# Shared products, shared additions and the first expert units in one fixed order; in the first layer half of the expert weights are loaded behind the base stores

## What is computed

```python
x = x + 0.5 * ffn(layernorm(x))
x = x + attention(layernorm(x))
x = x + 0.5 * ffn(layernorm(x))

def moe(x, router_w, w_gate, w_up, w_down, ws_gate_up, ws_down):   # E = 64 experts, K = 8, F = 96, C = 64
    probs = softmax(x @ router_w.T)
    topk_w, topk_ids = top_k(probs, K);  topk_w /= sum(topk_w)
    # each expert takes its first C tokens in token order, the others are dropped
    g = einsum('ecd,edf->ecf', xb, w_gate);  u = einsum('ecd,edf->ecf', xb, w_up)
    y = einsum('ecf,efd->ecd', silu(g) * u, w_down)
    routed = segment_sum(y[slot of (token, expert)] * topk_w, token)
    gu = x @ ws_gate_up;  shared = silu(gu[:, :SF]) * gu[:, SF:] @ ws_down   # SF = 96
    return routed + shared
```

## Time and profile before

| | us |
|---|---|
| median of 3 runs | 890.02 |
| lowest and highest of them | 889.1, 890.67 |
| the profiled execution, its whole time | 890.89 |
| the span of its trace | 889.1 |
| first layer: start of the first and of the last unit's scatters | 87.67, 187.08 |
| second layer: the same | 774.02, 874.78 |

### The profile page before, as it was taken

One profiled execution on the slowest core, in us unless ns is written; L12 is line 12 of the kernel. 1 busy time (PEld: TensorE's weight loads), 2 busy tenths in 40 slices (PEclk: granted clock), 3 DMA queues, 4 the chain that ended last, 5 costly groups with the idle time before them and its releaser, 6 DMA issues.

```text
span 889.1 us, 17025 instructions
## 1 busy us (share of the span) xinstructions
PE 675.8 (76%) x5060; PEld 310.2 (35%) x5121; DVE 606.8 (68%) x1572; ACT 461.0 (52%) x1060; POOL 389.1 (44%) x509
## 2 busy tenths in 40 slices
PE   4886567503799999999999999999970388577650
PEld 3644444402133333333333333332220264354430
DVE  4877644344978888888888888888813569754430
ACT  5742222201177777777777777777773675222310
POOL 5546787676431331331331331330004655677762
PEclk9996778655599999999999999999995559657865
DMA  6996443243424444444444444434110131544324
GB/s 185 254 232 188 78 72 62 37 103 63 89 56 99 91 84 100 86 82 100 84 83 100 85 82 101 85 81 102 26 36 18 37 89 52 146 79 66 62 33 107
DMA packets 233724, 80.26 MB, mean 90 GB/s; under 512 B 166888, under 2 KB 226440, under 8 KB 233608
## 3 DMA queue, kind: packets, MB, share of 16 engines
q1 hardware_dynamic: 212936, 64.94, 33.0%
q0 software_dynamic: 12288, 10.49, 8.1%
q10 hardware_dynamic: 8448, 4.20, 1.6%
HBM read 49.94 MB, written 31.49 MB: 92 GB/s over the span
## 4 chain that ended last, share of the span: by engine, by line
PE 49%; issue 11%; DVE 9%; POOL 8%; DMA 7%; ACT 7%; another core or an unknown queue 1%; POOLq 0%; ACTq 0%; SPq 0%; DVEq 0%
PE psum L1453 14%; PE psum L1444 12%; PE psum L1431 10%; DMA sums<-sums_sb,sidx 6%; ACT arena L1203 5%; POOL sums L623 4%; PE psum L1263 1%; PE psum L1407 1%; PE psum L1265 1%; POOL arena L600 1%; PE psum L1272 1%; PE psum L1393 1%; PE psum L1249 1%; PE psum L1421 1%
## 5 line engine op out<-in xcount | busy, mean ns | idle before, releaser
L984 DVE TENSOR_REDUCE arena<-psum 128x2 f32<-128x1024 f32 x256 | 308.8, 1220 | 53.1 <-PE psum L1431 50.2
L1203 ACT ACTIVATE arena<-psum 128x512 f32<-128x512 f32 x512 | 282.1, 600 | 116.1 <-PE psum L1444 105.7
L1431 PE MATMUL psum<-arena 126*128 126x512 bf16 x512 | 198.8, 395 | 8.9 <-DVE arena L984 4.5
L1444 PE MATMUL psum<-arena 128*128 128x512 bf16 x451 | 173.2, 387 | 7.1 <-ACT arena L1203 3.4
L1453 PE MATMUL psum<-arena 128*32 128x512 f32 x1024 | 136.2, 604 | 1.3 <-ACT arena L1194 1.3
L679 POOL CAST arena<-arena 128x256 bf16<-128x256 f32 x32 | 12.7, 396 | 264.9 <-issue 260.9
L623 POOL DMA_INDIRECT sums<-sums_sb,sidx x64 | 102.9, 1607 | 58.5 <-DVE sums_sb L919 33.1
L1444 PEld LDWEIGHTS psum<-arena 128*128 128x128 bf16 x512 | 50.7, 100 | 150.1 <-ACT arena L1203 122.3
L919 DVE COPY sums_sb<-psum 128x256 f32<-128x256 f32 x32 | 13.6, 425 | 95.5 <-DMA sums<-sums_sb,sidx 55.7
L600 POOL DMA_INDIRECT arena<-dispatch_rows,arena x64 | 64.8, 1013 | 20.7 <-issue 18.3
L1431 PEld LDWEIGHTS psum<-arena 126*128 126x128 bf16 x512 | 49.6, 99 | 37.8 <-DVE arena L984 15.0
(11 more groups left out here) (138 smaller groups left out, 1095.8 us busy)
## 6 DMA issues: line engine op xcount, KB each, us to landing
arena<-qk_parts SPq DMA_DIRECT2D x128, 96.0 KB
ctx<-arena SPq DMA_DIRECT2D x32, 256.0 KB, 2.0
qk_parts<-arena SPq DMA_DIRECT2D x32, 192.0 KB, 3.8
dispatch_rows<-xn_sb ACTq DMA_DIRECT2D x16, 256.0 KB, 2.3
arena<-lists SPq DMA_DIRECT2D x16, 256.0 KB
sums<-x_sb SPq DMA_DIRECT2D x16, 256.0 KB
arena<-qk_parts SPq DMA_DIRECT2D x64, 64.0 KB
arena<-ctx SPq DMA_DIRECT2D x64, 64.0 KB, 2.4
```

What stands on the lines that cost most here:

```text
L984: dve.tensor_reduce(mx_r[r % 2][:, 2 * p:2 * p + 2], src, X, ALU.max).then_inc(a_mx, 1)
L1203: act.activation(p_r[tau % NPB], bank[4 + tau % 2][:, :], ACT.Exp, scale=SCALE).then_inc(a_P, 1)
L1431: ins = pe.matmul(bank[tau % 4][:, :], heads(q_st[r], rows, g)[:, qt * P:(qt + 1) * P], heads(k_st[r], rows, g), start=True, stop=True)
L1444: pe.matmul(bank[4 + tau % 2][:, :], keys, heads(q_st[r], rows, g), start=True, stop=True)\
```

## The change

It does five things, in both layers unless said otherwise.

1. POOL takes `shared_add(0)` to `shared_add(4)` from DVE. They stand between the products: `shared_mul(g)`, then `shared_add(g - 2)`. DVE keeps groups 5, 6 and 7, with a semaphore of their own. `shared_mul(0)` moves ahead of the last group's `weights`.
2. POOL's gathers all stand behind the products and additions. Six are issued, then POOL waits until PE has finished `gate_up(1)`, then two more; `ahead(q)` is 8 + 2q, so twelve units have gathers behind their scatters.
3. PE's `places(0)` moves behind `up(7)`, and `places(1)` one unit earlier.
4. DVE's order in the unit stage: `match` ahead of `hidden` and of `sum_copy`, `merge_blocks(1)` ahead of the loop, the other list steps a unit earlier and behind `pick`. `match` gets a third buffer `same`.
5. First layer only: the expert weights are loaded in slices of eight experts (gate, up, down). The first twelve transfers (experts 0 to 31) go between the stores of routing; the other twelve are issued by SP behind the base stores and `load_rows(1)`. PE waits for the first twelve before the units and for the others before `gate_up(4)`. The loads of the attention weights move from ahead of `load_rows(2)` to behind it.

The diff, cut to its core:

```diff
-        same = [carve(3 * P) for _ in range(2)]
+        same = [carve(3 * P) for _ in range(3)]
...
-                w, t = ((w_gate, wgu_sb[:, :, 0:F]), (w_up, wgu_sb[:, :, F:2 * F]), (w_down, wd_sb))[c // 8]
-                part = slice(c % 8 * E // 8, (c % 8 + 1) * E // 8)
+                w, t = ((w_gate, wgu_sb[:, :, 0:F]), (w_up, wgu_sb[:, :, F:2 * F]), (w_down, wd_sb))[c % 3]
+                part = slice(c // 3 * E // 8, (c // 3 + 1) * E // 8)
...
-                        expert_weights(2 * g)
-                        expert_weights(2 * g + 1)
+                        for c in range(12 * g // NG, 12 * (g + 1) // NG):
+                            expert_weights(c)
                     store_w(NG - 1, 1)
-                    for c in range(2 * NG, 24):
-                        expert_weights(c)
...
                 for c in range(1, 4):
-                    if c == 2 and f.p == 0:
+                    if c == 3 and f.p == 0:
                         attention_weights()
                     wait(sp, f.gtp, 2 * c - 1)
                     load_rows(c)
+                    if c == 1 and f.p == 0:
+                        for w in range(12, 24):
+                            expert_weights(w)
...
+                def shared_add(g):
+                    wait(pool, f.shy, g + 1)
+                    xs = x_sb[:, g * GT:(g + 1) * GT, :]
+                    pool.tensor_tensor(xs, xs, z_sb[:, g * GT * P:(g + 1) * GT * P].rearrange("p (i d) -> p i d", i=GT),
+                                       ALU.add).then_inc(f.shx.sem, 1)
...
+                    if g == NG - 1:
+                        shared_mul(0, 0)
                     weights(g, g % 2)
...
-                gather(0)
-                shared_mul(NG - 2, 0)
-                gather(1)
-                shared_mul(NG - 1, 1)
-                ahead = lambda q: min(NP2, 10 + 2 * q)
-                for k in range(2, ahead(0)):
+                ahead = lambda q: min(NP2, 8 + 2 * q)
+                for k in range(6):
+                    gather(k)
+                wait(pool, f.gu, 2)
+                for k in range(6, ahead(0)):
                     gather(k)
...
-                    wait(dve, f.sm, q - 1)
+                    wait(dve, f.sm, q - 2)
...
-                places(0)
                 up(NG - 2, 0)
                 down(NG - 3, 1)
                 up(NG - 1, 1)
+                places(0)
...
+                    if q == 4:
+                        pe.wait_ge(s_wexp[1], 16 * 12)
```

71 lines of the change are left out of this document (37 added, 34 removed).

## The result

| | kernel before | changed kernel |
|---|---|---|
| median, first comparison (20 runs each) | 890.94 us (886.71 to 894.07) | 893.15 us (890.47 to 898.3) |
| ratio, 95% interval | | 1.0032 (1.0017 to 1.0047) |
| second comparison (run 5 below): ratio | | 1.0050 (1.0033 to 1.0067) |
| spans of two traces each | 889.1, 888.4 us | 889.4, 891.9 us |

The changed kernel is slower, by 0.3 to 0.5%. The forecast was 884.4 us, with a range from 880.0 to 892.5. The changed kernel's first profiled execution took 891.11 us and lies on its quick side; the second, at 893.64, is close to its medians (893.15 and 893.03). Those of before took 890.89 and 890.13, the first at its median of the first comparison (890.94), both above its medians in the later ones (886 to 888 us).

What follows compares the result with a forecast made beforehand. POOL's scatters and gathers were taken to pace the two expert layers' units (6.42 us a period); first scatters, gathers, stalls and collision sum to -5.6 us, from the median of 890.0 to 884.4 us, range 880.0 to 892.5.

Steps and rivals of the forecast that it cites:

- The late weights: First layer: last twelve transfers, 4.7 MB, take 16 to 19 us, end at about 93, covered before `match(4)` and `gate_up(4)`.
- The collision: First layer: scatters of units 0 and 1 run beside full DMA engines, +1.5 us.
- rival 2: First layer: weights under 220 GB/s make list rows late for `match(4)`; at 150 GB/s unit 2 waits about 10 us, 894; chance 0.10.
- ACT's wait for `silu(1)`: Before the first scatters, both layers: ACT's idle 5.00 and 4.03 us ahead of `silu(1)` was taken as gone.
- the sum: Both layers: first scatters -3.3 and +0.8, gathers +0.6 twice, stalls -3.0 and -2.8, collision +1.5: -5.6 us.
- My path of 18.8 us: Both layers: from indices ready to the first scatters, 18.8 us, so scatters start at 84.4 and 774.8.
- Rival 1: Both layers: ACT's wait before `silu(1)` stays, first scatters 2.2 and 2 to 6.4 us later; 888.6 to 893; chance 0.22.
- Contention of list steps: List stage: DVE's short steps wait for POOL, 3 to 4.5 us per list; indices 4.2 us later in second layer.
- The merge ahead of the first `sum_copy`: Before the first scatters, both layers: the merge comes into the path, 2.85 us.
- Stalls of units 1 and 3: Unit stage: their waits for `sum_copy` beyond the 0.3 us gap go, -3.0 us first layer, -2.8 second.
- Eight gathers ahead: Unit stage: one more period has gathers, +0.6 us per layer; about 1 us of slack before the scatters.
- rival 3: Unit stage: eight gathers ahead are too few, 0.4 us more in each of 24 periods; 894; chance 0.05.

Runs made afterwards that it cites:

- run 5: The changed kernel again, unaltered, timed against the kernel before: ratio 1.0050 (1.0033 to 1.0067).
- runs 10: Changed kernel with POOL's five additions back on DVE: 1.0078 of before; the same with all weights ahead and the merge behind the first `sum_copy`: 0.9971.
- run 11: The kernel before with only the five additions moved to POOL, between its products: ratio to before 1.0085 (1.0057 to 1.0112).
- Run 9: Changed kernel with all weights loaded where before has them and second-half list steps behind the first `sum_copy`; run twice: 0.9941 and 0.9942 of before.
- run 1: The changed kernel with all expert weights transfers where the kernel before has them: ratio to before 1.0015 (0.9999 to 1.0031).
- run 12: The kernel before with only DVE's unit order and third buffer `same`, merge and list steps unmoved: 0.9923 of before, 881.25 us against 887.9.
- run 13: Two variants of run 9: attention weights loaded behind the last list rows, 0.9969 of before; ten gathers ahead instead of eight, 0.9977.
- run 2: The kernel before with only part 5 of the change, the late weights: ratio to before 1.0048 (1.0024 to 1.0072).

## Why the prediction was wrong

- **The late weights**: the step that failed most. The collision was put at +1.5 us (bounds 0 to 6), the transfers at 16 to 19 us, ending at about 93. The units of the first layer took 2.5 us more where -0.9 was forecast, and the part alone costs 4.3 us (0.48%). The rate was wrong: the 4.7 MB took 25.7 us in the first trace, until 99.07, and 25.7 to 28.5 us in all six, so 165 to 184 GB/s. The 244 to 301 GB/s of the earlier trace rows are what all transfers of a 2 us stretch moved; the same trace had the nearer row, 199 GB/s for its last eight transfers. I had the rows land just behind 93 and `match(4)` want them at 95, "covered by 2 us only". They were issued at 94.1, `match(4)` ran at 99.9, and DVE had been ready for it since 91.9, earlier than I said. This is rival 2, by its own condition (under 220 GB/s), and I gave it 0.10. Its mechanism came as written, `match(4)` and `sum_copy(2)` behind it, but at 3.2 us of unit 2 and not 10.
- **ACT's wait for `silu(1)`**: taken as gone, and it was, but it was never the kernel's. In the second trace of before, from the indices to the first scatter is 20.05 and 20.07 us, not 22.4 and 22.2. The changed kernel needs 19.6 to 19.7 in all four cases, so it gains 0.4 there, not the 3.4 to 3.6 of the sum (1.5 against the mean of both traces). This is the second failed step: a gain counted from a stall of one execution. My path of 18.8 us was also 0.8 short; a wait of `hidden(0)` for `silu(0)`, 0.9 to 1.1 us in the four cases, was not in it. The two together make up the misses of 1.9 and 2.0 us up to unit 0. Rival 1 feared the stall would stay; that it came by chance was in no rival.
- **Contention of list steps**: right in kind, and in size against the mean: indices 4.3 us later in the second layer (forecast 4.2), +0.2 in the first (+0.4). What the whole part is worth depends on POOL's order, as runs 10 and 11 show.
- **The merge ahead of the first `sum_copy`**: its 2.9 us were in my path of 18.8, so the forecast holds it. I didn't ask what it buys. Run 9 against run 1: it costs 0.7%, and no run shows a gain from it.
- **Stalls of units 1 and 3**: right where nothing else comes between. In the first layer a wait of 2.42 us for unit 0's scatters took the place of unit 1's. In the second layer the units took 2.8 us less (forecast 2.2), and run 12 shows that the gain comes with DVE's order alone.
- **Eight gathers ahead**: right as far as the time shows (run 13). In the traces unit 2 of the second layer comes 0.8 to 2 us late with them, where I had up to 2 us to spare: rival 3 in small, at one unit and not in every period.

Put together: DVE's order gains 0.8%; with the additions and the gathers of POOL some 0.6% are left (run 9; the two aren't told apart). The merge ahead of `sum_copy` takes 0.7%, and the late weights 0.2 to 0.35% more (from run 1 to the two figures of the changed kernel; the interval of the first figure overlaps run 1's, that of the second doesn't).

## What to carry to other kernels

When transfers are moved within one queue, what stands behind them waits: list the first user of each, and price the load by how long a comparable load took from its first issue to its last landing, not by what all DMA engines moved in a short stretch. Call it covered only when the margin is larger than what the same step varies by from one trace to the next. A stall that the trace puts down to nothing should be looked for in a second trace before its disappearance is counted as a gain. And when a change has five parts, price each one for what it buys too: here one part alone beats the whole.

## What the runs showed that I had not expected

- A single trace of this kernel is uncertain by about 2 us in a stretch of 140: the second layer from keys to unit 15 took 138.6 and 140.0 us in two traces of before, and 136.1 in run 2, whose order of instructions is the same there. Gains of this size need two traces or a timed comparison.
- What held the late `silu(1)` of the first trace stays open. The Trainium skill says in Runtime: NRT & Kernel Launch, Instruction fetch mechanics, that an engine fetches its instructions by DMA ahead of use and that this is mostly hidden. Seventeen of eighteen traces agree, with `silu(1)` at most 1.20 us after the engine's last work. For the other one a late fetch is only a guess: a packet of an instruction queue moves at 768.12 in the second layer's wait (765.89 to 769.92), but none moves in the first layer's (78.68 to 83.68).
- A group of four short list steps can be blocked by more than one POOL instruction: the group that takes 0.49 us took 2.72 in the second trace of the changed kernel and 3.67 in run 11.
